# Two pairs of lanes per stage in the routed-expert loop, scatters two pairs later, and one shared-expert block moved into the loop's last turning

## The reference, cut to what matters

```python
logits = flat @ router_w                                   # 2048 x 64 experts
_, topk_idx = jax.lax.top_k(logits + router_bias, 4)
...
g = silu(einsum('nd,edf->nef', flat, wg))                  # e = 64 experts, f = 128
u = einsum('nd,edf->nef', flat, wu)
routed = einsum('ne,nef,efd->nd', comb, g * u, wd)         # comb: 4 nonzero weights a token
sg = silu(einsum('nd,sdh->nsh', flat, swg))                # s = 2 shared experts, h = 512
su = einsum('nd,sdh->nsh', flat, swu)
shared = einsum('nsh,shd->nd', sg * su, swd)
return x + (routed + shared)
```

## Time and profile before

| | us |
|---|---|
| median of 3 runs | 1094.67 (1093.06 to 1094.89) |
| the profiled execution | 1093.33 |
| its span, first to last instruction | 1091.5 |
| PE busy (share of the span) | 1044.1 (96%) |
| DVE | 847.6 (78%) |
| ACT | 660.4 (61%) |
| POOL | 531.5 (49%) |

### The profile page before, as it was taken

How to read it: one execution, slowest core, us unless ns; L and a number is a source line. 1 busy time by engine, 2 the same in 40 slices (tenths; PEclk the granted TensorE clock), 3 DMA queues, 4 the chain that set the end, 5 groups by cost and what they waited for, 6 DMA issues and landing times.

```text
span 1091.5 us, 29734 instructions
## 1 busy us (share of the span) xinstructions
PE 1044.1 (96%) x9833; PEld 504.9 (46%) x9833; DVE 847.6 (78%) x1331; ACT 660.4 (61%) x1334; POOL 531.5 (49%) x540
## 2 busy tenths in 40 slices
PE   5998899999999999899999999999999999989998
PEld 3534333333333333345544456666666666634443
DVE  5976999999999997398878927676767676758283
ACT  3323688888888889735620317777777777712020
POOL 6631143334333433435871947777777888610000
PEclk9998999999999999999999999999999999989999
DMA  9164121122112210044200077878887698458261
GB/s 259 27 169 106 36 56 46 46 70 61 44 44 72 59 44 25 5 151 155 78 1 1 2 272 246 268 269 276 313 284 237 228 319 294 170 197 264 66 226 39
DMA packets 72409, 150.66 MB, mean 138 GB/s; under 512 B 19460, under 2 KB 20868, under 8 KB 72356
## 3 DMA queue, kind: packets, MB, share of 16 engines
q1 hardware_dynamic: 52404, 109.51, 31.4%
q0 software_dynamic: 18304, 38.86, 10.7%
q10 hardware_dynamic: 1648, 1.58, 0.4%
HBM read 223.90 MB, written 38.80 MB: 241 GB/s over the span
## 4 chain that ended last, share of the span: by engine, by line
PE 71%; DVE 16%; issue 7%; ACT 3%; DMA 1%; POOL 1%; DVEq 0%; SPq 0%; ACTq 0%; POOLq 0%
PE PS L1483 17%; PE PS L1360 14%; PE PS L1465 8%; DVE maxes L1558 6%; PE PS L1502 6%; PE PS L1274 6%; PE PS L1223 4%; DVE max_low L1558 4%; PE PS L1155 4%; PE PS L1443 3%; PE PS L1252 3%; ACT att L1004 2%; PE PS L1327 2%; PE PS L1444 2%; DMA w_att<-in_L_attn_wq_dram 1%
## 5 line engine op out<-in xcount | busy, mean ns | idle before, releaser
L1004 ACT ACTIVATE att<-PS 128x512 f32<-128x512 f32 x576 | 312.5, 595 | 52.3 <-PE PS L1252 45.5
L1274 PE MATMUL PS<-att,v_head 128*32 128x256 f32 (+1 forms) x2560 | 178.8, 370 | 0.9 <-POOL att L793 0.9
L1558 DVE TENSOR_REDUCE maxes<-PS 128x2 f32<-128x1024 f32 (+2 forms) x192 | 172.7, 938 | 2.0 <-PE PS L1160 1.8
L1360 PE MATMUL PS<-XN,att 128*128 128x512 f16 x768 | 169.1, 382 | 0.3 <-ACT w_att L1066 0.3
L1558 DVE TENSOR_REDUCE max_low<-PS 128x2 f32<-128x1024 f32 x128 | 153.1, 1207 | 5.3 <-PE PS L1155 3.2
L919 POOL DMA_INDIRECT w_att<-xn_rows,idx x96 | 117.6, 1225 | 47.0 <-DVE w_att L1882 12.5
L793 POOL TENSOR_SCALAR_AFFINE_SELECT att<-att 128x512 f32<-128x512 f32 (+1 forms) x96 | 74.9, 787 | 127.9 <-ACT att L1004 127.1
L1252 PE MATMUL PS<-att 50*128 50x512 f16 (+1 forms) x640 | 112.2, 364 | 14.2 <-ACT att L1004 11.8
L1155 PE MATMUL PS<-att 48*128 48x512 f16 (+7 forms) x768 | 116.2, 327 | 8.8 <-DVE max_low L1558 3.8
L1360 PEld LDWEIGHTS PS<-XN,att 128*128 128x128 f16 x768 | 75.2, 98 | 92.1 <-issue 3.9
L1062 ACT ACTIVATE w_att<-PS 128x512 f32<-128x512 f32 x32 | 19.1, 598 | 159.6 <-PE PS L1360 159.6
(11 more groups left out here) (205 smaller groups left out, 1825.7 us busy)
## 6 DMA issues: line engine op xcount, KB each, us to landing
ring<-in_L_ffn_wg_dram SPq DMA_DIRECT2D x96, 512.0 KB
XT<-in_L_ffn_wg_dram SPq DMA_DIRECT2D x96, 512.0 KB
ring<-in_L_ffn_wd_dram SPq DMA_DIRECT2D x96, 256.0 KB
XT<-in_L_ffn_wd_dram SPq DMA_DIRECT2D x96, 256.0 KB
ring<-choice_y SPq DMA_DIRECT2D x16, 1024.0 KB, 7.2
att<-q_stacks SPq DMA_DIRECT2D x60, 128.0 KB, 2.5
xn_rows<-ring SPq DMA_DIRECT2D x16, 256.0 KB, 3.3
out_dram<-X SPq DMA_DIRECT2D x16, 256.0 KB, 6.8
```

The source lines that it names most:

```text
L1004: act.activation(probs[:, n0 % RING, u * BANK:(u + 1) * BANK], bank((2 * n0 + u) % EXP_BANKS), ACT.Exp, scale=HD ** -0.5 / QK_SCALE ** 2). ...
L1274: mm = pe.matmul(PS[32 * r:32 * r + 32, at:at + qn], v_head[b][:, kt, :], probs[:, (NS * b + s) % RING, a:a + qn], start=s in (0, NS0), st ...
L1360: mm = pe.matmul(bank(2 * (n % 2) + k), shared_w[:, 2 * k + w, C * s + c, at:at + P], v[:, c, tokens], start=(c == 0 and w == 0 and v is x ...
L1558: last = dve.reduce_max(out, src, AXX)
```

## The change

Each engine's `expert_pairs` handles two pairs (a, a+1) per stage in place of one. PE does both slot turns (of a+2 and a+3), both hidden turns (of a-2 and a-1), both ups, both downs. ACT and DVE are written in a new order to match. The split down weights have four buffers instead of two and lie in the first half of `x_hi` (the tokens of the early groups, which are no longer needed). The indices of pair n+6 are handed out in stage n, two at a time, where those of pair n+5 were before, and only once the slot turns that free the gather buffer are done. A scatter follows its gather by ten pairs instead of eight. The slot turns of pair 1 move ahead of the last early `shared_down` tile. In the last turning, PE does `shared_up(2, 0)` (unit 16) between the downs of pairs 92, 93 and the hidden turns of pairs 94, 95.

```diff
-        down_hi, down_lo = carve_all(flat_xt, 2 * W, *[([P, 2, 2 * D], F16)] * 2)
+        down_hi, down_lo = x_hi[:, :, 0:2 * D], x_lo[:, :, 0:2 * D]
...
-            for i in range(2):
+            for i in range(3):
                 for j in range(JP):
                     gather_tokens(i, j)
-            with pool.Fori(2, LANE_TILES) as i:
+                    if i == 2 and j >= 2:
+                        scatter_y(0, j - 2)
+            with pool.Fori(3, LANE_TILES) as i:
                 for j in range(JP):
                     gather_tokens(i, j)
-                    scatter_y(i - 2, j)
-            for i in range(LANE_TILES - 2, LANE_TILES):
-                for j in range(JP):
-                    scatter_y(i, j)
+                    scatter_y(i - 3 + j // 2, (j - 2) % JP)
+            for n in range(PAIRS - 10, PAIRS):
+                scatter_y(n // JP, n % JP)
...
-            def expert_pairs(i, first, last):
-                for j in range(JP):
-                    n = JP * i + j
-                    if not (last and j == JP - 1):
-                        turned_tokens(n + 1, j + 1)
-                    if not (first and j < 2):
-                        hidden_turned(n - 2, (j - 2) % JP)
-                    if not last:
-                        next_tokens(i + 1 + (j + 1) // JP, (j + 1) % JP)
-                    if not (first and j < 1):
-                        down_high(n - 1, (j - 1) % JP, i if j else i - 1)
-                    silu(n, j)
-                    e_high(n, j)
+            def expert_pairs(i, first, turns, gathers):
+                for a in range(0, JP, 2):
+                    both = (a, a + 1)
+                    if not (first and a == 0):
+                        for j in both:
+                            hidden_turned(JP * i + j - 2, (j - 2) % JP)
+                    if a < gathers:
+                        for j in both:
+                            act.wait_ge(xg_turned, JP * i + j + 3)
+                            next_tokens(i + 1 + (j + 2) // JP, (j + 2) % JP)
+                    if not (first and a == 0):
+                        down_high(JP * i + a - 1, (a - 1) % JP, i if a else i - 1)
+                    for j in both:
+                        n = JP * i + j
+                        silu(n, j)
+                        if a < turns:
+                            turned_tokens(n + 2, j + 2)
+                        e_high(n, j)
+                    down_high(JP * i + a, a, i)
...
-                        turn_slots(0, 0, 0)
+                        for n in range(2):
+                            turn_slots(n, n, 0)
...
             def expert_pairs(i, first, last):
-                for j in range(JP):
-                    n = JP * i + j
-                    if not (last and j == JP - 1):
-                        turn_slots(n + 1, j + 1, i)
-                    if not (first and j < 2):
-                        turn_hidden(n - 2, (j - 2) % JP)
-                    expert_up(n, j, i)
-                    if not (first and j < 2):
-                        expert_down(n - 2, (j - 2) % JP)
+                for a in range(0, JP, 2):
+                    both = (a, a + 1)
+                    if not (last and a == JP - 2):
+                        for j in both:
+                            turn_slots(JP * i + j + 2, j + 2, i)
+                    if not (first and a == 0):
+                        for j in both:
+                            turn_hidden(JP * i + j - 2, (j - 2) % JP)
+                    for j in both:
+                        expert_up(JP * i + j, j, i)
+                    if not (first and a == 0):
+                        for j in both:
+                            expert_down(JP * i + j - 2, (j - 2) % JP)
...
-            turn_hidden(PAIRS - 2, JP - 2)
-            turn_hidden(PAIRS - 1, JP - 1)
-            expert_down(PAIRS - 2, JP - 2)
-            expert_down(PAIRS - 1, JP - 1)
+            pe.wait_ge(xgt_ready, PAIRS)
+            pe.wait_ge(x_lo_ready, 4 * (EARLY + 1))
+            shared_up(EARLY, 0)
+            for j in (JP - 2, JP - 1):
+                turn_hidden(PAIRS - JP + j, j)
+            for j in (JP - 2, JP - 1):
+                expert_down(PAIRS - JP + j, j)
 
             for g in range(EARLY, 4):
-                shared_ups(g, g % EARLY)
+                shared_ups(g, 1)
                 shared_down(g)
...
-            def expert_pairs(i, first, last):
-                for j in range(JP):
-                    n = JP * i + j
-                    expert_hidden(n, j)
-                    if not (first and j < 1):
-                        down_low(n - 1, (j - 1) % JP)
-                    e_low(n, j)
-                    if not (first and j < 2):
-                        expert_y(n - 2, (j - 2) % JP, i if j >= 2 else i - 1)
+            def expert_pairs(i, first):
+                for a in range(0, JP, 2):
+                    later = not (first and a == 0)
+                    n, before = JP * i + a, i if a else i - 1
+                    if later:
+                        down_low(n - 2, (a - 2) % JP)
+                        down_low(n - 1, (a - 1) % JP)
+                    expert_hidden(n, a)
+                    e_low(n, a)
+                    expert_hidden(n + 1, a + 1)
+                    if later:
+                        expert_y(n - 2, (a - 2) % JP, before)
+                    e_low(n + 1, a + 1)
+                    if later:
+                        expert_y(n - 1, (a - 1) % JP, before)
```

47 lines of the change are left out of this document (25 added, 22 removed).

## The result

The kernel after took 1085.28 us (median of 6 runs, 1083.92 to 1086.71) beside 1093.87 (6 runs, 1092.27 to 1094.89) of the kernel before on the same chip: ratio 0.9929, 95% interval [0.9914, 0.9943]: 7.8 us less by the ratio, 8.6 by the medians. In a later set it was run again: 1085.42 beside 1093.26, 0.9928 [0.9906, 0.9950]. I had said 1083.0 in a range of 1080.5 to 1090. The profiled execution took 1084.45 us over a span of 1082.7.

What follows compares the result with a forecast made beforehand. PE was taken to bound the loop, with empty seams where the kind of matmul changes. Loop -13.4 and turning +1.9 gave -11.5 us: 1081.8 against the profiled execution, 1083.2 against the median, said as 1083; range 1080.5 to 1090.

Steps and rivals of the forecast that it cites:

- What bounds the kernel: Routed loop: PE sets the pace at 3.207 us a pair, 0.28 of it empty seams; two-pair stages take 6.13 us.
- The loop's sum: From the end of the early shared block to the last ups issued: 305.1 us before, 291.7 after, 13.4 less.
- U: Time at which the last ups are issued, zero of the clock for the last turning; 955.14 before.
- gathers and weights: Loop transfers: gathers begin 7.3 us ahead of need, weight loads 10.5 instead of 11.1; no cost counted for either.
- The turning: Behind the last ups: the moved shared block gains nothing, unit 19 starts later; +1.9 us, between +0.7 and +2.9.
- the wait before unit 19: Late shared block, fourth unit: PE idles 3.9 us because mix(0) blocks shared_hidden(17) on DVE, until U + 24.8.
- A part lost: Rival, loop: PE waits some 0.15 us per stage for e_low or a second gather, 7 us: 1090; chance 0.16.
- The change doesn't pay: Rival, loop: seams not halved or POOL keeps its present pace, stage 6.42 us: 1096, or 1094; chance 0.07.
- Slower, both writebacks stop POOL in full: Rival, loop: two disturbances make POOL need 6.6 us per stage, 9 us plus the tail: 1105; chance 0.07.
- What disturbs POOL: Loop: a DVE writeback lengthens an overlapping POOL instruction from 1.01 to 1.67 us; one disturbance, 0.66, counted per stage.
- one of my signs: POOL's rows in the loop: at most one of four instructions longer than 1.3 us.
- my fourth rival: Both writebacks stop POOL in full, so POOL needs 6.6 us per stage: 1105; chance 0.07.

Runs made afterwards that it cites:

- early hand-out: Changed kernel with ACT's index copies for both pairs put ahead of the copies of the turned hidden rows: 1083.59 us, 0.9912 of the kernel before.
- three edits: Changed kernel with late mix, early hand-out and turn first together: 1078.74 us, 0.9866 of the kernel before.
- extra seams: Changed kernel with one more full-width 128x128 fp16 matmul between the two ups of each stage: 1096.90 us, 1.0045 of the kernel before.
- Block back: Changed kernel with the last turning's shared block (unit 16) put back behind the last downs: 1082.15 us, 0.9903 of the kernel before.
- gathers first: Changed kernel with POOL doing a stage's two gathers, then its two scatters: 1086.89 us, 0.9956 of the kernel before.
- turn first: Changed kernel with the last two hidden turns ahead of the shared block instead of behind it: 1084.16 us, 0.9921 of the kernel before.
- late mix: Changed kernel with every DVE mix one shared unit later: 1082.69 us, 0.9895 of the kernel before.

## Why the prediction was right, point by point

- **What bounds the kernel** (PE's own pace, with empty seams where the kind of matmul changes): shown. Halving the seams gave 6.14 us a stage (predicted 6.13), and putting one round of them back by itself gave 6.45.
- **The loop's sum**, -13.4: the term that was mis-sized. U came 9.7 us earlier in the first profile (955.14 to 945.42) and 6.6 in the second (948.55). In the first, 3.1 us of the difference are the surplus of seven stages, about 0.4 is the stage (6.14 and not 6.13, 45 times), 0.1 is stage 1 and 0.1 the start of the loop. The step that failed is the one on gathers and weights: "I take nothing, since a late gather would have had to use up the whole 9.1 before", and "I count nothing" for the weights. I had a gather begin 7.3 us ahead of its turn at the least. Taking the gathers and the slot turns of the trace in order, the shortest lead was 8.9 us before and 5.8 after, and the gathers that PE waited for in the two profiles after had begun 6.0 to 8.0 us ahead. So a gather does take up to 8 us at times, which 8.9 hid and 5.8 doesn't. With the early hand-out the shortest lead is 7.1 and no gather is late. The rest, seen in the three edits, is a weight load. I had also read the free DMA share of 22% as room, but it was a mean over 300 us: in 10 us windows the share was up to 1.00 before and after.
- **The turning**, +1.9: 0.9 measured in the profile (U to end, 136.4 to 137.3), and -0.2 in the second. The chain up to the last writeback came out within 0.05 us. From there to the first mix it took 8.90 us (8.79 in the second profile) where I had 9.99 + 0.35, so the first mix was 1.4 us earlier than said, and the wait before unit 19 2.2 us (1.2 in the second) instead of 3.9. Right in its core: the block in the gap gains nothing, the wait moves to where the mix blocks DVE. "Gains nothing" was probably too kind: without the move the kernel took 2.7 us less, at the edge of the noise. Two pairs per stage shorten the last turning even without a block in it (PE idle 1.97 us and not 3.08), which I had not worked out.
- **The number.** 1083 beside 1085.3 is partly luck: I took 3.7 us too much from the loop and added 1.0 too much in the turning, and the two errors offset each other in part.
- **The rivals.** "A part lost" is partly true: 3 to 7 us over the loop, though not as 0.15 us in each stage but in a few stages, for DMAs. "The change doesn't pay" is refuted on these chips by the stage and the extra seams. "Slower, both writebacks stop POOL in full" did not come, and its mechanism was wrong (next point).
- **What disturbs POOL.** I wrote that the disturbed instruction overlaps a writeback and the free one doesn't. POOL's and then DVE's timeline after say otherwise:

```profile
885.06 1.03 POOL L919 DMA_INDIRECT w_att<-xn_rows,idx  x1 [0.30 <-issue]
886.39 2.08 POOL L928 DMA_INDIRECT choice_y<-att,idx_y  x1 [0.31 <-issue]
888.78 1.86 POOL L919 DMA_INDIRECT w_att<-xn_rows,idx  x1 [0.30 <-issue]
```

```profile
884.91 0.68 DVE L1900 TENSOR_SCALAR w_att<-PS 128x512 f32<-128x512 f32 x1
...
885.77 0.68 DVE L1900 TENSOR_SCALAR w_att<-PS 128x512 f32<-128x512 f32 x1
886.37 1.21 DVE L1891 SCALAR_TENSOR_TENSOR XN<-XT,XN 128x1024 f16<-128x1024 f32 x1
888.51 1.23 DVE L1891 SCALAR_TENSOR_TENSOR XN<-XT,XN 128x1024 f16<-128x1024 f32 x1 [0.93 <-ACT XN L1110]
```

  The gather at 885.06 meets two writebacks and takes 1.03. The scatter at 886.39 starts 0.02 after a `down_low` and takes 2.08; the gather at 888.78 starts 0.27 after one and takes 1.86. So a POOL instruction loses what is left of a running `down_low`, less some 0.1. Between 660 and 940 us this holds for all 86 that began during one before and all 50 after (less 0.10 to 0.16 us each), and none of the 49 that began during a writeback after took over 1.04. It also broke one of my signs: of the four POOL instructions from 885.06 to 890.95, two and not at most one are longer than 1.3. The disturbed gather of before, 1.67 at 934.42, fits too: the DVE timeline there has `down_low` running from 933.97 for 1.22. The Trainium skill (SBUF — State Buffer, "Who interferes with whom") says that a DVE instruction with two inputs in SBUF contends with a GpSimd instruction that reads SBUF, which is `down_low`; that sentence, and not the one on tensor_scalar that I had taken, is the one that bears on this kernel. By it my fourth rival had no ground: POOL was busy 228.9 us in the loop before and 213.7 after.

## What to carry to other kernels

Look for the places where PE changes between full width and two halves, or between fp16 and fp32: here they cost 0.28 us for each round of changes with nothing in the profile waiting, and doing two of each kind in a row gave all of the 0.7% that the kernel gained. When a stage is shortened, work out the shortest lead of every transfer in it, and read the DMA share in windows as short as a few stages, since the mean over the loop hides the stretches in which a transfer takes longest. Before filling a gap in a turning, ask what stands behind the longest chain: here the filler delayed the chain by 5 us, while putting one blocking consumer (the mix) behind a producer that others wait for was worth some 3 us.

## What the runs showed of the hardware

- In the profiles from one chip, over half of PE's signals behind `expert_up` came more than 1.7 us late in three kernels, the latest by 3.5 or more (in the fourth, the early hand-out, most were on time, and those behind the slot turns were late instead). The same kernel before took 1178 us on it and 1092 to 1094 elsewhere. Block back was 1.0% faster than before elsewhere (0.9903) and 1.4% slower there (1.0135), while the early hand-out, 0.1% from it elsewhere (0.9912), was 4% faster there (0.9589). Whether an edit pays can depend on the chip.
- An indirect DMA on POOL takes 0.99 to 1.04 us alone and up to 2.08 when it starts just behind a DVE instruction of 128x1024 with both inputs in SBUF, one fp32 and one fp16 (`down_low`). The DVE instruction is not lengthened (1.21 to 1.23 us), and a 128x512 writeback out of PSUM disturbs nothing.
- The granted clock fell to its lower level in or just behind a PE wait of 1.6 to 2.5 us in the last turning in the profiles of before, of both runs of after, and of extra seams, gathers first and turn first, each time for 3.4 us (about 6.9 before). In the early hand-out the same waits, 1.59 and 2.31 us, brought no fall, nor did the 1.59 in the late mix and the 1.50 in block back.
